# The third layer's first norm inside the second layer's last steps, and the first layer's diagonals on ScalarE

## The chip, the cores and the metric

The kernel runs on one core of one Trainium2 chip, in one launch. The metric is the device time of that launch in microseconds, the median of several runs. A profile of one execution stands beside it. The engines are TensorE (PE, with its weight loads as PEld), VectorE (DVE), ScalarE (ACT), GpSimd (POOL) and SyncE (SP), which here issues the plain DMAs.

## The reference

Four layers work on x of 4096 tokens by 256 values. Each normalises x and adds two branches, an attention and a feed-forward one:

```python
def _layernorm(x, axis=-1, eps=1e-05):
    m = jnp.mean(x, axis=axis, keepdims=True)
    v = jnp.var(x, axis=axis, keepdims=True)
    return (x - m) / jnp.sqrt(v + eps)
...
    x = L0_attn_x
    xn = _layernorm(x, axis=-1)
    x = x + _L0_attn_ref(xn, ...) + _L0_ffn_ref(xn, ...)
    xn = _layernorm(x, axis=-1)
    x = x + _L1_attn_ref(xn, ...) + _L1_ffn_ref(xn, ...)
...
```

The attention of the first layer is gated linear attention: a state per head, `S = S * exp(g_t) + k_t v_t`, read by `q_t @ S`. Its feed-forward branch is a mixture of 8 experts, the best two for each token:

```python
        w, idx = jax.lax.top_k(gate_logits, TOP_K)
        w = jax.nn.softmax(w, axis=-1)
...
        out = jnp.einsum('nec,ne->nc', y, comb)
```

The second layer has a selective scan (mamba) and a layer of retrieved experts (PEER, with rows gathered from tables). The third has a retention, whose core is a sigmoid of a product and a scan, with a feed-forward net behind it, and beside it a net of binary weights:

```python
        sig = jax.nn.sigmoid(jnp.einsum('bsh,hk->bsk', x, W_ret) + b_ret)

        def ema_step(carry, s_t):
            xi = 0.5 * s_t + 0.5 * carry
            return (xi, xi)
...
        w = jnp.where(kernel_bool, jnp.float32(1.0), jnp.float32(-1.0))
        return x @ w
```

The fourth is causal attention with 16 heads, and a root of two squared products.

## The kernel before

x stays on the chip, transposed: `xT` holds 128 partitions by 2 halves by 4096 tokens, and is worked on in 8 blocks of 512 tokens (`NB`, `BW`). Each layer is a function that returns one program for each engine. A program weaves the two branches of its layer: generators give their steps in turn, and where each step goes is set by paces (`weave`, L155; in the first layer `on_clock`, L168, through `weave_layer`, L508), in the second and third by tables of slots (`AT`, L1424 and L1979). So each engine's order is fixed when the program is built. At the end of a layer every engine goes through `layer_end` (L384), which waits for the last tick of every stage of the layer; SyncE issues the loads of the next layer behind it. Nearly all products go through one helper, `chain`, at L184, so that line stands for most of TensorE's rows.

**First layer's end.** The last expert tile is written to memory (`ys_slots`), and then the results come back by token: for each of `NC` = 32 groups of 128 tokens SyncE fetches two rows per token into `Gy` (L531, 8 buffers), and TensorE adds the two, weighted, with a product by a diagonal matrix for each: `wd`, 18 buffers of [128, 2, 128]. The diagonals are `ident` times a weight from `w8`. GpSimd makes them (L1288), one instruction for a pair, as soon as the last expert product (`y`, `TILES - 1`) is done, since `Gy` and `wd` lie in the memory `FW` in which the experts' weights were. VectorE adds the result to x (L1070). The last steps of the linear attention run in between: VectorE's `S` update (L857), TensorE's products, ScalarE's copies of `ob` (L1128), squares (L1134), gates (L1140), logarithm and exponential (L1146, L1150).

**Second layer's end.** Block 7 of the scan ends with `out_of(7)`: on TensorE a product of `u` with `mWo`, two halves of 4 matmuls each, which the trace shows as 16 passes; on VectorE two additions of it to x (L1605) and two of the residual (L1610). Behind it comes the last token group of PEER: transposes of `hg` (L1571), products with `hgT` and with diagonals made on ScalarE (L1866), and VectorE's weighted sums (L1764) and last addition to x (L1776). PSUM has three banks for this branch, `psm`, used in turn.

**Third layer's start.** Behind the barrier SyncE loads rW, vec, k0, W1, W2 and k1 in this order (L2043 to L2048). The norm of blocks 0 and 1 goes one step after another over three engines: sum of the two halves (L2009, VectorE), mean by a product with `onesm` (L1998, TensorE), subtraction (L2014), squares (L2028, ScalarE), their sum (L2019), variance (L2004, TensorE), table load, logarithm, exponential (L2035 to L2040, ScalarE), scaling (L2023, VectorE; that of block 1 behind the first scans). Then come the cast of x to `xa` (L2286), the signs of k0 (L2057, read from `bh`), the product with rW, the sigmoid (L2337) and the scan (L2193). The norms of later blocks stand inside the loop over blocks and aren't touched. Buffers: `sqs` were `sq_` and a part of `fa`; `both_` held the half sums.

## Time and profile before

| | us |
|---|---|
| median of 3 runs | 3743.24 |
| lowest, highest | 3740.03, 3744.06 |
| profiled execution | 3738.18 |
| its span | 3736.0 |

The profile is of one execution, and its moments are counted from the start of the span; what lies around the span in that run is 2.18 us. The mean granted clock of TensorE over the span is 0.962. TensorE is busy for 93% of the span, VectorE for 66%, ScalarE for 46% and GpSimd for 32%. Such shares are means over four layers with different limits. What a change in one place is worth is read from that place: the chain of work that ended last gives, step by step, what each piece of time was spent on, and the timeline what the other engines did beside it. The number in brackets behind a row is the time in which its engine was idle before it, with what ended that.

### The profile page before, as it was taken

What the parts mean: (1) busy time and instruction counts of PE and PEld (TensorE: products, weight loads), DVE (VectorE), ACT (ScalarE), POOL (GpSimd) and SP (SyncE); (2) the same over time, 40 slices, a digit from 0 to 9 for tenths busy, and PEclk for the clock granted to TensorE, in tenths of its full rate; (3) what the DMA queues carried; (4) which work ended last, traced back from release to release, by engine and by line L of the source; (5) the groups of instructions that cost most, each with busy time, mean ns of one, the idle gap of its engine ahead of it and who ended that gap; (6) DMA issues with size and microseconds to landing.
All of it is one profiled execution on the core that took longest, in us unless ns stands there. A gap on an engine that the chain in (4) does not pass through costs nothing.

```text
span 3736.0 us, 48136 instructions
## 1 busy us (share of the span) xinstructions
PE 3458.4 (93%) x16660; PEld 2069.5 (55%) x16660; DVE 2456.5 (66%) x6314; ACT 1727.1 (46%) x3243; POOL 1193.7 (32%) x1229
## 2 busy tenths in 40 slices
PE   9889999998999998999879999999799999999998
PEld 6556778776555555555546677777443333433332
DVE  5553344344799999999965434443568888788884
ACT  3333442332334433344334544444247676667667
POOL 0023334332455556555632322322221111011111
PEclk9889999999999999999989999999899999999999
DMA  2014555544476667766740000000111111111100
GB/s 81 33 61 154 186 186 189 183 141 169 150 216 203 209 203 219 214 203 208 233 148 3 1 1 1 1 0 1 44 22 29 25 26 34 33 31 31 35 18 23
DMA packets 105971, 368.88 MB, mean 99 GB/s; under 512 B 26736, under 2 KB 39680, under 8 KB 95744
## 3 DMA queue, kind: packets, MB, share of 16 engines
q0 software_dynamic: 58000, 303.74, 25.2%
q1 hardware_dynamic: 46640, 59.98, 5.8%
q8 instruction: 132, 2.16, 0.2%
q10 hardware_dynamic: 1088, 2.10, 0.2%
q14 instruction: 111, 0.91, 0.1%
HBM read 322.59 MB, written 17.69 MB: 91 GB/s over the span
## 4 chain that ended last, share of the span: by engine, by line
PE 70%; DVE 18%; ACT 7%; issue 3%; POOL 1%; DMA 1%; POOLq 0%; DVEq 0%; SPq 0%; ACTq 0%
PE ps L184 54%; PE ps L2710 6%; DVE mi L1687 2%; ACT P L2991 2%; PE ps L1552 2%; DVE hacc L1727 2%; DVE gathB L1764 2%; DVE pm L2858 2%; PE ps L2171 1%; DVE mx L1683 1%; PE ps L594 1%; DVE tm L1641 1%; DVE ps L2861 1%; PE ps L619 1%; PE ps L584 1%
## 5 line engine op out<-in xcount | busy, mean ns | idle before, releaser
L2991 ACT ACTIVATE P<-ps 128x512 f32<-128x512 f32 (+3 forms) x1280 | 587.9, 545 | 202.5 <-PE ps L184 200.2
L2858 DVE TENSOR_REDUCE pm<-ps 128x1 f32<-128x512 f32 x768 | 485.0, 683 | 72.9 <-PE ps L184 68.0
L1905 POOL DMA_INDIRECT gathB<-in_tab,idx x256 | 286.5, 1119 | 313.7 <-PE ps L1552 243.5
L184 PE MATMUL ps<-KS,QS 63*128 63x512 f32 (+3 forms) x1280 | 341.7, 412 | 16.8 <-ACT P L2991 5.5
L3048 POOL TENSOR_SCALAR_AFFINE_SELECT P<-P 128x256 f32<-128x256 f32 x256 | 102.9, 407 | 675.5 <-ACT P L2991 670.0
L1905 POOL DMA_INDIRECT gathA<-in_tab,idx x256 | 267.7, 1046 | 152.0 <-issue 77.4
L2710 PE MATMUL ps<-P,Va 128*32 128x512 f32 (+3 forms) x2560 | 302.7, 545 | 7.1 <-POOL P L3048 4.2
L184 PE MATMUL ps<-QS,KS 64*128 64x512 f32 (+3 forms) x1280 | 281.6, 423 | 1.5
L184 PEld LDWEIGHTS ps<-QS,KS 64*128 64x128 f32 x1280 | 131.6, 186 | 253.9 <-ACT P L2991 104.1
L2861 DVE CUSTOM_DVE_ANT_0 ps<-ps,past 128x128 f32<-128x128 f32 (+3 forms) x512 | 240.8, 513 | 36.3 <-PE ps L184 33.2
L184 PEld LDWEIGHTS ps<-KS,QS 63*128 63x128 f32 x1280 | 158.0, 186 | 168.5 <-ACT P L2991 80.4
L184 PE MATMUL ps<-f,K 128*128 128x512 f32 x1024 | 249.3, 395 | 0.0
L184 PE MATMUL ps<-WS,xn 128*128 128x512 f32 x512 | 231.2, 592 | 0.0
L184 PEld LDWEIGHTS ps<-f,K 128*128 128x128 f32 x1024 | 192.2, 188 | 46.8
L184 PE MATMUL ps<-moe,FW 128*128 128x128 f32 x1704 | 203.9, 277 | 0.8 <-ACT moe L1218 0.8
L184 PEld LDWEIGHTS ps<-moe,FW 128*128 128x128 f32 x1704 | 198.0, 194 | 1.1 <-ACT moe L1218 1.0
L1764 DVE CUSTOM_DVE_ANT_0 gathB<-hg,gathB,gte 128x512 f32<-128x512 f32 x256 | 178.1, 748 | 1.0 <-DMA gathB<-in_tab,idx 1.0
L1727 DVE SCALAR_TENSOR_TENSOR hacc<-gathA,lin,hacc 128x512 f32<-128x512 f32 x224 | 167.1, 746 | 3.5
L2432 POOL TENSOR_TENSOR f<-fa,f 128x512 fp32r<-128x512 f32 x64 | 85.3, 1333 | 258.8 <-DVE f L2304 258.8
L1246 POOL DMA_INDIRECT FW<-in_F,fidx x71 | 72.5, 1022 | 284.3 <-DVE moe L1051 156.0
L1057 DVE TENSOR_TENSOR moe<-moe,ps 128x384 f32<-128x384 f32 x71 | 39.3, 554 | 180.3 <-PE ps L184 116.6
L184 PEld LDWEIGHTS ps<-WS,xn 128*128 128x128 f32 x512 | 95.5, 190 | 111.4 <-issue 106.2
(392 smaller groups left out, 6952.2 us busy)
## 6 DMA issues: line engine op xcount, KB each, us to landing
FW<-ys_slots SPq DMA_DIRECT2D x32, 256.0 KB, 3.4
KS<-hi SPq DMA_DIRECT2D x256, 32.0 KB, 1.9
QS<-hi SPq DMA_DIRECT2D x256, 32.0 KB, 1.9
gathA<-in_tab,idx POOLq DMA_INDIRECT x256, 5.5
gathB<-in_tab,idx POOLq DMA_INDIRECT x256, 5.1
KS<-lo SPq DMA_DIRECT2D x128, 32.0 KB, 1.9
QS<-lo SPq DMA_DIRECT2D x128, 32.0 KB, 1.9
out<-xT SPq DMA_DIRECT2D x8, 512.0 KB, 3.2
```

The source lines that it names most:

```text
L184: m = pe.matmul(out, w, x, start=start and i == 0, stop=stop and i == len(pairs) - 1, skip_group_check=True)
L1552: pe.matmul(p[:, ms], GB[:, h, 512 + m * 128:640 + m * 128], dg[h], start=False, stop=h == 7, skip_group_check=True).then_inc(*PR.pe.tick( ...
L1687: v = dve.max_index(mi[:, 4 * g + i, :], mx[:, 4 * g + i, :], p[:, i * 128:(i + 1) * 128])
L1727: dve.scalar_tensor_tensor(out=hacc[:, :], in0=GA[:, h, 256:768], scalar=lin[:, h:h + 1], in1=src, op0=ALU.mult, op1=ALU.add).then_inc(*(P ...
L1764: dve.tensor_tensor_reduce(out=GB[:, h, 0:512], in0=hg[:, :], in1=GB[:, h, 0:512], scale=gt_[:, h:h + 1], scalar=0.0, op0=ALU.mult, op1=AL ...
L1905: pool.indirect_dma_start(out=(GA, GB)[half][:, h, :], out_offset=None, in_=d[f"tab{half}"], in_offset=bass.IndirectOffsetOnAxis(ap=idx[t ...
L2432: pool.tensor_tensor(f2[m % 2][:, 1, :], fa[:, (m + 2) % 3, :], f2[m % 2][:, 0, :].bitcast(F32), ALU.subtract).then_inc(*BN.pool.tick("f2" ...
L2710: m = pe.matmul(o_[32 * hd:32 * hd + 32, off:BW], Va[:, kt, h * 17:h * 17 + 32], Pb[2 * (kt % 2) + hd // 2][:, hd % 2, off:BW], start=kt = ...
L2858: v = dve.tensor_reduce(m, p, AX.X, ALU.max)
L2861: v = dve.tensor_tensor_reduce(out=p, in0=p, in1=past[:, 512 - w:512], scale=1.0, scalar=-3.0e38, op0=ALU.add, op1=ALU.max, accum_out=m)
L2991: act.activation(P_[:, hh, off:BW], psx.tile("s2", j, n, kt, pr, hh)[:, off:BW], ACT.Exp).then_inc(*psx.emptied(MN.act, "s2", j, n, kt, pr ...
L3048: pool.affine_select(out=P_, in_=P_, compare_op=ALU.is_ge, fill=0.0, base=0, pattern=[[0, 2], [1, 128]], channel_multiplier=-1).then_inc(* ...
```

## The change

It has two parts. In the first layer the diagonals are made by ScalarE, with two instructions for a pair in place of one of GpSimd, and are put at points of ScalarE's program between the attention's last steps, 14 groups ahead of their use. In the second and third, the norm of the third layer's blocks 0 and 1 is spread over the end of the second layer: the half sums in slot 8 of block 7, means and subtractions ahead of `out_of(7)`, sums of squares between its two additions, variances behind it, squares, roots and scalings at the ends of the programs of their engines. The buffers `both`, `xa`, `bh` and a new `rfirst` are placed in memory that is free by then. TensorE's program of the third layer begins with a wait for the logarithm of block 1.

```diff
@@ -768,7 +768,7 @@
                     p = psf.fill("moe", c)
                     pe.wait_all(psf.freed("moe", c))
                     for i in range(2):
-                        pe.wait_ge(*FF.pool.has("weight", c + i))
+                        pe.wait_ge(*FF.act.has("weight", c + i))
@@ -1229,8 +1229,23 @@
...
-                yield from delay(AFTER)
-                for _ in range(0, NC, 2):
+
+                def weights(c):
+                    act.wait_ge(*FF.dve.has("wb"))
+                    act.wait_ge(*FF.pe.has("y", TILES - 1))
+                    for i in range(c, c + 2):
+                        act.wait_ge(*FF.pe.has("moe", i - NWD))
+                        for s in range(2):
+                            a = act.activation(wd[i % NWD][:, s, :], ident[:, :], ACT.Copy, scale=w8[:, 2 + s, i:i + 1])
+                        a.then_inc(*FF.act.tick("weight", i))
+
+                yield from delay(1)
+                for c in range(0, 2 * AFTER - 2, 2):
+                    weights(c)
+                    yield
+                for c in range(0, NC, 2):
+                    if c + 2 * AFTER - 2 < NC:
+                        weights(c + 2 * AFTER - 2)
                     yield
 
@@ -1281,12 +1296,6 @@
...
-                pool.wait_ge(*FF.dve.has("wb"))
-                pool.wait_ge(*FF.pe.has("y", TILES - 1))
-                for c in range(NC):
-                    pool.wait_ge(*FF.pe.has("moe", c - NWD))
-                    pool.tensor_tensor(wd[c % NWD], ident[:, :].rearrange("p (o t) -> p o t", o=1).broadcast_to([128, 2, 128]),
-                                       w8[:, 2:4, c:c + 1].broadcast_to([128, 2, 128]), ALU.mult).then_inc(*FF.pool.tick("weight", c))
@@ -1510,7 +1519,9 @@
...
+                layers[2]["first means"][0](pe, psm)
                 out_of(NB - 1)
+                layers[2]["first variances"](pe, psm)
@@ -1605,6 +1616,8 @@
...
+                        if (n, m) == (NB - 1, 0):
+                            layers[2]["first rests"](dve)
@@ -1628,6 +1641,10 @@
...
+                    if n == NB - 1:
+                        dve.wait_ge(*PR.pe.has("rt", NT - 5, 3))
+                        dve.wait_ge(*PR.pe.has("hid", NT - 5))
+                        layers[2]["first halves"](dve)
@@ -1672,6 +1689,7 @@
...
+                layers[2]["first means"][1](dve, psm)
                 out_of(NB - 1)
@@ -1786,6 +1804,7 @@
...
                 weave((dve_mamba(dve), RATIO, LATE), (dve_peer(dve), 1.0))
+                layers[2]["first scales"](dve)
                 layer_end(dve, *names)
@@ -1848,6 +1867,7 @@
...
+                layers[2]["first squares"](act)
@@ -1897,6 +1917,7 @@
...
                 weave((act_mamba(act), RATIO, LATE), (act_peer(act), 1.0))
+                layers[2]["first roots"](act, psm)
                 layer_end(act, *names)
@@ -1928,7 +1949,13 @@
...
             xn = sb("xn2", [128, 2, 3 * BW])
+            both_ = sb("both", [128, BW])
             Wr = sb("rW", [128, 2, 256])
+            ph1 = ExitStack()
+            first = alloc(ph1)("rfirst", [128, 2, 2, BW])
+            ph1.close()
+            xa = sb("xa", [128, 2, 2, BW], F32R)
+            bh = sb("bh", [128, 2, BW])
@@ -1955,7 +1979,8 @@
...
-            sqs = [sq_, fa[:, 0:2, :]]
+            halves = [both_[:, :], bh[:, 0, :]]
+            sqs = [first[:, i, :, :] for i in range(2)]
@@ -1989,6 +2014,55 @@
                         yield
...
+            def pe_first_means(pe, ps):
+                for n in range(2):
+                    p = ps.fill("next", n, "mu")
+                    pe.wait_ge(*K.dve.has("ones"))
+                    pe.wait_ge(*LN.dve.has(n, "half"))
+                    pe.wait_all(ps.freed("next", n, "mu"))
+                    pe.matmul(p[:, :], onesm[:, :], halves[n], start=True, stop=True).then_inc(*LN.pe.tick(n, "mu"))
+
+            def pe_first_vars(pe, ps):
+                for n in range(2):
+                    p = ps.fill("next", n, "var")
+                    pe.wait_ge(*LN.dve.has(n, "rest"))
+                    pe.wait_all(ps.freed("next", n, "var"))
+                    pe.matmul(p[:, :], onesm[:, :], sqs[n][:, 0, :], start=True, stop=True).then_inc(*LN.pe.tick(n, "var"))
+
+            def dve_first_halves(dve):
+                for n in range(2):
+                    dve.wait_ge(*x_before(n))
+                    dve.tensor_tensor(halves[n], blk(xT, 0, n), blk(xT, 1, n), ALU.add).then_inc(*LN.dve.tick(n, "half"))
+
+            def dve_first_means(dve, ps):
+                for n in range(2):
+                    dve.wait_ge(*LN.pe.has(n, "mu"))
+                    dve.tensor_tensor(xr2(n), both(xT, n), ps.tile("next", n, "mu")[:, None, :].broadcast_to([128, 2, BW]),
+                                      ALU.subtract).then_inc(*ps.emptied(LN.dve, "next", n, "mu"))
+
+            def dve_first_rests(dve):
+                for n in range(2):
+                    dve_rest(dve, LN, (n,), sqs[n])
+
+            def dve_first_scales(dve):
+                for n in range(2):
+                    dve_scale(dve, LN, (n,), xr2(n), sqs[n])
+
+            def act_first_squares(act):
+                for n in range(2):
+                    act.wait_ge(*LN.dve.has("next", n, "mu"))
+                    act.activation(sqs[n], xr2(n), ACT.Square).then_inc(*LN.act.tick(n, "sq"))
+
+            def act_first_roots(act, ps):
+                for n in range(2):
+                    act.wait_ge(*LN.pe.has(n, "var"))
+                    if n == 0:
+                        act.preload_act_table_set(LN_EXP)
+                    act.activation(sqs[n][:, 0, :], ps.tile("next", n, "var")[:, :], ACT.Ln, bias=epsc[:, 0:1]).then_inc(
+                        *ps.emptied(LN.act, "next", n, "var"))
+                    act.wait_ge(*LN.act.has("next", n, "var"))
+                    act.activation(sqs[n][:, 0, :], sqs[n][:, 0, :], ACT.Exp, scale=-0.5).then_inc(*LN.act.tick(n, "rstd"))
@@ -2174,10 +2248,7 @@
...
-                for n in range(2):
-                    pe_mean(pe, LN, (n,))
-                for n in range(2):
-                    pe_var(pe, LN, (n,), sqs[n])
+                pe.wait_ge(*LN.act.has("next", 1, "var"))
@@ -2201,7 +2272,6 @@
...
                 scan(0)
-                dve_scale(dve, LN, (1,), xr2(1), sqs[1])
                 dve.wait_ge(*RT.act.has("W1"))
@@ -2312,12 +2382,6 @@
...
             def dve(dve):
-                for n in range(2):
-                    dve_half(dve, LN, (n,), both(xT, n), [], [LN.pe.has(n - 1, "mu")])
-                    dve_mean(dve, LN, (n,), both(xT, n), xr2(n), [])
-                dve_rest(dve, LN, (0,), sqs[0])
-                dve_rest(dve, LN, (1,), sqs[1])
-                dve_scale(dve, LN, (0,), xr2(0), sqs[0])
                 dve_split(dve, 0)
                 dve_signs0(dve)
@@ -2403,10 +2467,7 @@
...
                 table.clear()
-                for n in range(2):
-                    act_squares(act, LN, (n,), xr2(n), sqs[n], [])
-                for n in range(2):
-                    act_root(act, LN, (n,), sqs[n])
+                table["now"] = LN_EXP
```

ScalarE, the end of the first layer; `FW` is where `wd` lies, `ob`, `rms` and `gsil` are the attention's. Minus is before, plus is now:

```order
-L1128 ACTIVATE ob<-ps 128x4x128 x2
+L1239 ACTIVATE FW<-ident,w 128x128 x8
+L1128 ACTIVATE ob<-ps 128x4x128
+L1239 ACTIVATE FW<-ident,w 128x128 x16
+L1128 ACTIVATE ob<-ps 128x4x128
+L1239 ACTIVATE FW<-ident,w 128x128 x8
 L1134 ACTIVATE rms<-ob 128x512 x2
-L1140 ACTIVATE gsil<-ps 128x512 x4
+L1140 ACTIVATE gsil<-ps 128x512 x2
+L1239 ACTIVATE FW<-ident,w 128x128 x4
+L1140 ACTIVATE gsil<-ps 128x512 x2
+L1239 ACTIVATE FW<-ident,w 128x128 x12
```

Between the attention's copies, squares and gates there now stand groups of 4 to 16 diagonals.

VectorE, the end of the second layer and the start of the third, before:

```order
L1776 TENSOR_TENSOR xT<-xT,ps 128x2x128
L1605 TENSOR_TENSOR xT<-xT,ps 128x512 x2
L1610 TENSOR_TENSOR xT<-xT,xn 128x512 x2
L1764 ISA gathB,lin<-hg,gathB,gte 128x512
...
L1776 TENSOR_TENSOR xT<-xT,ps 128x2x128
L2009 TENSOR_TENSOR both<-xT 128x512
L2014 TENSOR_TENSOR xn<-xT,ps 128x2x512
L2009 TENSOR_TENSOR both<-xT 128x512
L2014 TENSOR_TENSOR xn<-xT,ps 128x2x512
L2019 TENSOR_TENSOR rsq<-rsq 128x512
L2019 TENSOR_TENSOR fa<-fa 128x512
L2023 TENSOR_TENSOR xn<-xn,rsq 128x2x512
```

and now (`rfirst` is the squares' buffer):

```order
L1794 TENSOR_TENSOR xT<-xT,ps 128x2x128
L2041 TENSOR_TENSOR xn<-xT,ps 128x2x512 x2
L1616 TENSOR_TENSOR xT<-xT,ps 128x512
L2093 TENSOR_TENSOR rfirst<-rfirst 128x512 x2
L1616 TENSOR_TENSOR xT<-xT,ps 128x512
L1623 TENSOR_TENSOR xT<-xT,xn 128x512 x2
L1782 ISA gathB,lin<-hg,gathB,gte 128x512
...
L1794 TENSOR_TENSOR xT<-xT,ps 128x2x128
L2097 TENSOR_TENSOR xn<-xn,rfirst 128x2x512 x2
L2356 CAST xa<-xn 128x1024
L2131 TENSOR_TENSOR K<-bh 128x1024 x2
```

The subtractions and the sums of squares moved ahead of the additions to x, and behind the last addition only the two scalings are left before the cast.

TensorE, the same place, before:

```order
L184 MATMUL ps<-u,mWo 128x512 x8
L1571 MATMUL ps<-ident,hg 128x128 x4
L184 MATMUL ps<-hgT,pWo 128x128 x4
L1552 MATMUL ps<-dg,gathB 128x128 x4
...
L1552 MATMUL ps<-hg,gathB 128x128 x4
L1998 MATMUL ps<-both,onesm 128x512 x2
L2004 MATMUL ps<-rsq,onesm 128x512
L2004 MATMUL ps<-fa,onesm 128x512
L184 MATMUL ps<-xn,rW 128x512 x4
```

and now:

```order
L1563 MATMUL ps<-hg,gathB 128x128 x4
L2024 MATMUL ps<-both,onesm 128x512
L2024 MATMUL ps<-bh,onesm 128x512
L184 MATMUL ps<-u,mWo 128x512 x8
L2031 MATMUL ps<-rfirst,onesm 128x512 x2
L1582 MATMUL ps<-ident,hg 128x128 x4
L184 MATMUL ps<-hgT,pWo 128x128 x4
...
L1563 MATMUL ps<-hg,gathB 128x128 x4
L184 MATMUL ps<-xn,rW 128x512 x4
```

The means stand ahead of the product with `mWo`, the variances behind it, and the third layer's first product on TensorE is the one with `rW`.

## Rows read from the trace of the kernel before

**Rows 1.** The page's part 4: engines' shares of the chain that ended last.

```profile
PE 70%; DVE 18%; ACT 7%; issue 3%; POOL 1%; DMA 1%; POOLq 0%; DVEq 0%; SPq 0%; ACTq 0%
```

**Rows 2.** The chain in order of time, first layer's end: start us, us, what.

```profile
842.12 9.34 issue
...
853.51 17.55 PE ps L184 x96
```

**Rows 3.** Timeline, VectorE and GpSimd there: start us, busy us, engine, line, operation, out<-in.

```profile
834.30 0.62 DVE L857 SCALAR_TENSOR_TENSOR S<-S,ebe,U 128x128 f32<-128x128 f32 x2
...
841.61 10.39 POOL L1288 TENSOR_TENSOR FW<-ident,w 128x256 f32<-128x256 f32 x18
...
841.79 10.37 DVE L857 SCALAR_TENSOR_TENSOR S<-S,ebe,U 128x128 f32<-128x128 f32 x2
```

**Rows 4.** Windows there: us, busy (x) of PE, PEld, DVE, ACT, POOL; PEclk, DMA share, GB/s.

```profile
840.10:841.80 1.70, 1.70 (x17) 1.69 (x16) 1.41 (x5) 0.00 (x0) 1.17 (x2) 1.00 0.00 0
...
853.50:856.89 3.39, 3.38 (x16) 3.39 (x17) 1.92 (x6) 0.00 (x0) 0.00 (x0) 0.53 0.00 0
...
842.00:893.00 51.00, 34.97 (x160) 23.08 (x159) 24.31 (x28) 11.98 (x19) 18.06 (x30) 0.87 0.34 106
```

**Rows 5.** Timeline, ScalarE at the first layer's end; in brackets the idle time before.

```profile
857.09 0.60 ACT L1128 ACTIVATE ob<-ps 128x512 f32<-128x512 f32 x1 [14.40 <-PE ps L184]
```

**Rows 6.** Tile FW (gathers), 835 to 860: issue to landing.

```profile
DMA to landing us min/median/max: 2.5/4.2/5.5
```

**Rows 7.** The chain in order of time, second layer's last block.

```profile
1834.41 3.33 DVE tm L1641 x5
```

**Rows 8.** Timeline, the second layer's tail.

```profile
1908.82 10.10 PE L184 MATMUL ps<-u,mWo 128*128 128x512 f32 x16 [5.03 <-DVE u L1598]
...
1915.59 0.69 DVE L1605 TENSOR_TENSOR xT<-xT,ps 128x512 f32<-128x512 f32 x1 [3.49 <-PE ps L184]
...
1918.96 0.69 DVE L1605 TENSOR_TENSOR xT<-xT,ps 128x512 f32<-128x512 f32 x1 [2.67 <-PE ps L184]
...
1926.26 1.28 ACT L1866 ACTIVATE hg<-ident,lin 128x128 f32<-128x128 f32 x4 [2.29 <-DVE lin L1764]
...
1933.04 0.42 DVE L1776 TENSOR_TENSOR xT<-xT,ps 128x256 f32<-128x256 f32 x1 [6.81 <-PE ps L1552]
```

**Rows 9.** The chain in order of time, the third layer's start.

```profile
1952.44 1.24 DVE re L2193
...
1956.63 1.14 DVE xn L2023
...
1968.03 3.37 DVE K L2062 x2
```

**Rows 10.** Timeline of that stretch; the last row is from tile bh, min/median/max ns.

```profile
1934.40 0.43 SPq L2045 DMA_DIRECT2D bh<-in_k  x1
...
1935.57 1.22 DVE L2014 TENSOR_TENSOR xn<-xT,ps 128x1024 f32<-128x1024 f32 x1 [1.28 <-PE ps L1998]
...
1946.59 6.54 PE L184 MATMUL ps<-xn,rW 128*128 128x512 f32 x8 [2.32 <-DVE xn L2023]
...
1950.43 1.28 ACT L2337 ACT_TABLE_LOAD   x1 [3.96 <-PE ps L184]
...
L2057 DVE TENSOR_TENSOR K<-bh x2: 1217/2290/3364, 1947.1 to 1948.3; 128x1024 fp32r<-128x1024 uint8 x2
```

**Rows 11.** DMA issues, 1933 to 1985: KB each, us to landing.

```profile
raw<-in_k SPq DMA_DIRECT2D x1, 1024.0 KB, 10.4
...
bh<-in_k SPq DMA_DIRECT2D x1, 512.0 KB, 4.6
...
rW<-in_rWr SPq DMA_DIRECT2D x1, 256.0 KB, 2.5
```

**Rows 12.** Windows, TensorE's clock in layers 2 and 3 (columns of rows 4).

```profile
1908.82:1914.82 6.00, 6.00 (x7) 2.52 (x8) 3.18 (x8) 1.91 (x2) 4.78 (x5) 0.50 0.84 269
...
1960.60:1970.00 9.40, 8.31 (x20) 5.00 (x20) 6.08 (x5) 5.89 (x9) 3.60 (x2) 0.71 0.00 0
...
1982.15:2012.80 30.65, 30.65 (x125) 24.68 (x126) 10.53 (x15) 10.61 (x17) 6.25 (x4) 0.94 0.03 9
```


## What I expect of it

> **What bounds the kernel now.** I read the chain of work that ended last first, by engine, to see who sets the time: TensorE 70% of the span, VectorE 18%, ScalarE 7%, and "issue", 3%, in which an engine waited for nothing that the profile shows [rows 1]. GpSimd has 1%. So work that leaves GpSimd pays only where GpSimd holds up another engine, and work that moves ahead pays only where TensorE or VectorE stood waiting. Then I read the same chain in order of time around the two places that the change touches, and beside it the timeline, which shows what the other engines did in that moment.
>
> At the end of the first layer the chain has a hole: VectorE's first update of the state `S` takes its usual third of a microsecond, then come 9.34 us of "issue", and only then do the second update and 17.55 us of TensorE work follow [rows 2]. The timeline has that pair at 10.37 us where the same pair, 7 us earlier, took 0.62; and exactly beside it lie 18 GpSimd instructions, the diagonals, 10.39 us back to back, 0.58 each [rows 3]. At the change from the second layer to the third the chain goes step by step through one norm, from the last addition to x at 1933.04 to the first scan of the retention at 1952.44 [rows 8, 9]. The sum is made against the profiled execution (3738.18 us), 5.06 us under the median of 3743.24.
>
> **Part 1, diagonals on ScalarE.** *Removed:* 32 GpSimd instructions. With them the cover of the hole goes. The second update would follow the first at 842.12 and end 9.34 us earlier; with the first one's share of the pair's excess (10.37 − 0.62) it is 9.7 us. *What is late next* is TensorE's work that uses `S`: it then starts after a pause of about a microsecond and not of eleven. After the long pause its first 16 matmuls of 128x128 took 3.38 us at a granted clock of 0.53; 17 such ones right before the hole took 1.70 at 1.00 [rows 4]. That is 1.6 us more. Against it, the gathered expert rows `Gy` are now wanted earlier: a gather lands 2.5 to 5.5 us after its issue [rows 6], and the first are issued about a microsecond after the last expert product, just behind the new need of the first pair, for which I charge 0.3. Sum: −9.7 − 1.6 + 0.3 = **−11.0** (bounds −8.5, when the gathers are waited for by 2.8 us, and −12).
>
> *Added:* 64 ScalarE instructions of 128x128. The nearest row has four of them at 1.28 us, 0.32 each [rows 8]: 20 us in all. ScalarE is busy for 11.98 of the 51 us from 842 to 893 [rows 4], and stood 14.40 us before the copy of `ob` at 857.09 [rows 5]; the first 32 diagonals (10 us) fit there, in the time in which the hole stood. The rest lie between two normalising steps, where ScalarE delays one by 4 × 0.32 = 1.3 us at most while VectorE has work of its own. I take 0; if none of it were covered it costs 20 us, the upper end, as a rival below. The last ten pairs are TensorE's and stay as they are.
>
> By the Trainium skill ("SBUF — State Buffer", section "Who interferes with whom") VectorE with two SBUF inputs and GpSimd reading SBUF lock one port pair for a whole instruction, and the other blocks until that one is finished. Taken by its words the hole would be one GpSimd instruction long, and this part would be worth 0.6 instead of 9.7; the rows show the wait going on through 16 or so of them, so I follow the rows and keep the rule's result as the first rival.
>
> **Part 2, the norm inside the second layer's tail.** *Moved to VectorE's slot 8 of block 7:* two additions of 128x512 (`halves`), at 0.69 each by the row of the same shape [rows 8]: 1.4. VectorE is on the chain there: 3.33 us of `tm` at 1834.41 [rows 7], with TensorE waiting. So these count in full but for rounding: **+1.3** (0 to +1.4).
>
> *Moved to the tail, in program order:* two mean matmuls before the output product. TensorE idles 5.03 us before it [rows 8], and the means need only the halves: covered. Two subtractions of 128x1024, 1.22 each [rows 10], before the first x addition: VectorE idles 3.49 there, 2.4 covered. Two `rests` of about 0.69 between the two x additions: idle 2.67 [rows 8], covered. The squares on ScalarE come behind the last gelu and are done before the product is. The two variances stand on TensorE behind the output product, ahead of the transposes of `hg`: 1.1 to 1.7 us, and those transposes feed products that anyway wait for diagonals made by ScalarE at 1926.26, before which ScalarE idled 2.29. The roots (table load 1.28 [rows 10], two logarithms and two exponentials at 0.60, the row of the nearest ScalarE shape [rows 5]) come behind ScalarE's last diagonals at 1927.54 and end about 1931.3, before VectorE's last addition at 1933.04, for which VectorE idles 6.81 [rows 8]. I take **0** for all of it. Ends: +5 if subtractions, rests and variances all come onto the path (2.4 + 1.4 + 1.7, less the slack of one), and −3 if TensorE, now idle for only some 3.3 us ahead of the output product, keeps its full clock: the first 6.00 us of that product ran at 0.50 [rows 12].
>
> **Part 3, the third layer's start.** *Gone from the path:* halves, means, subtractions, squares, rests, variances, roots. What is left from the end of the last addition (1933.46): two scales (2 × 1.22) to 1935.9 and the cast to `xa`, 0.7, to 1936.6. From there two branches meet at the first scan. TensorE: the weights rW, issued at once after the barrier, land 2.5 us later [rows 11], 1936.1, so its product starts there. The first output takes 4 of the 8 passes that took 6.54 us [rows 10]; I take half and a little more, 3.8, since the first ran at the lower clock: 1939.9, then table load 1.28 and one sigmoid 0.7: 1941.9. VectorE: the signs of k0 (2 × 1.22 undisturbed) wait for a load issued at 1934.40 that lands after 4.6 us [rows 10, 11], 1939.0; one of the two was stretched to 3.36 beside GpSimd's own first step [rows 10]. GpSimd's step now starts before the load lands, so I leave 0.8 of that: 1942.3. The scan starts at 1942.4 and not at 1952.44 [rows 9]: −10.0. Behind the two scans the second block's scale, 1.14, has gone from the chain too [rows 9]: −11.1. *What is late next:* raw key bytes of 1024 KB land 10.4 us after issue [rows 11], 1946.5; they are first read 15.6 us behind the first scan's start, at 1968.03 [rows 9], in the new time near 1957. Sum **−11.1** (−8 if the loads, now the last to come, take 3 us more; −12 without GpSimd's disturbance). The rest of the third layer has the same order of instructions, so the shift stays.
>
> **Sum:** −11.0 + 1.3 + 0 − 11.1 = −20.8. In the profiled frame 3717.4; against the median 3743.24 − 20.8 = **3722.4**.
>
> **The rivals.**
>
> (a) *The hole isn't GpSimd's run.* Then something else that starts at the same moment holds `S`, the eight gathers for one, or GpSimd's part in it is one instruction, 0.6. For it: the gathers too are in flight in the hole. Against: the hole ends with the 18th diagonal, to 0.2 us. The first part gives 0.6: 3743.24 − 0.6 + 1.3 − 11.1 = 3732.8. This is also the case that the edit doesn't do what it says. Chance 0.10.
>
> (b) *The norm's steps come onto the path of the tail:* VectorE and TensorE there have idle times of 2.7 to 5.0 us, but each such idle ends the moment that a result comes, and a step that starts late pushes what follows. +5 and 2 us less at the handover: 3743.24 − 20.8 + 7 = 3729. Chance 0.14.
>
> (c) *TensorE stays warm* ahead of the output product: −3, 3719.4. Chance 0.08.
>
> (d) *ScalarE becomes the bound at the first layer's end:* its queue is in order, and diagonals that wait for a freed buffer hold up the normalising steps behind them. With all 20 us exposed, 3742.4. Against it: 39 us of idle in the window. Chance 0.04.
>
> (e) *Slower:* one mechanism, the clock. In the third layer's first block TensorE works at 0.71 from 1960.60 on and at 0.94 over 30.65 us from 1982.15 [rows 12]; the new timing of its pauses there could leave it at the lower level, 0.50, until the next one. 8.31 × (0.71/0.50 − 1) + 30.65 × (0.94/0.50 − 1) = 3.5 + 27 = 30.5 us: 3722.4 + 30.5 = 3753. It decides for slower once over 28 us are lost. Against it: the pauses ahead of that stretch get shorter, not longer. Chance 0.02.
>
> **How the numbers follow.** My forecast, all three sums about as above, has the remaining 0.62. The likeliest time is 3722.4. Its own bounds are 3743.24 − 12 − 2 − 12 = 3717 and 3743.24 − 8.5 + 5 − 8 = 3732; runs of the same kernel lie up to 3 us from the median, so the range begins at 3714. It ends at 3733 to take in (a) and (b); only (d), (e) and the outsides are left out. A measurement of this kernel can tell 0.2% from no change, 7.5 us: faster means below 3735.7. Forecast, (a), (b) and (c) lie below it, 0.94 together, but (a) and (b) at once would give about 3740, for which I take off 0.02: faster 0.92, same 0.06, slower 0.02.
>
> **What would show it.** Step 1 is right if the two updates of `S` take 0.6 to 0.7 us, with no "issue" of several us behind the first, and the 16 matmuls behind them run at a clock near 1.0; wrong, by (a), if the pair is still near 10 us, and by (d) if TensorE's products of the last pairs wait for ScalarE's diagonals. Step 2 is right if the second layer's tail from the start of the output product to the last x addition takes as long as before (1908.82 to 1933.04, 24 us); wrong by (b) if the subtractions stand in the chain. Step 3 is right if the first scan starts 9 us after that last addition and not 19. If k0's signs stand in the chain with a wait for the load of over 4.6 us, the loads were the term that I mis-sized.

## The result, and the profile after

| | before | after |
|---|---|---|
| median us | 3741.64 (3732.95 to 3747.90, 6 runs) | 3715.43 (3714.22 to 3724.15, 6 runs) |
| ratio after / before | | 0.9936, 95% interval 0.9924 to 0.9947 |
| profiled execution us | 3738.18 | 3724.15 |
| its span us | 3736.0 | 3722.4 |

The change makes the kernel 0.64% faster (0.53% to 0.76%), 26.2 us by the medians (0.4 us of it outside the span, 2.2 us before and 1.8 after). A second measurement, of 6 and 13 runs, gave 3718.32 against 3740.74, a ratio of 0.9940 (0.9926 to 0.9953), 22.4 us. The forecast was 20.8 us less, 3722.4; its range, 3714 to 3733, holds both.

The profiled execution of after is the slowest of its six, 8.7 us above their median, so one profile alone would tell of 13.6 us. To see where time goes I compare the start of the same TensorE matmul, by its number in the program, in two traces; "lag" is after less before. The kernel was profiled once more (`again`, below), and its parts alone.

| lag us at | after | again | diag_only | norm_only | run_held |
|---|---|---|---|---|---|
| 826, ahead of the hole | +5.8 | −0.7 | +0.1 | −0.1 | −0.3 |
| 860, behind it | −4.9 | −11.7 | −10.7 | −0.1 | −10.6 |
| 917, second layer's start | −4.8 | −11.4 | −10.5 | −0.1 | −10.6 |
| 927, 10 us later | −1.5 | −8.1 | −7.2 | −0.1 | −10.6 |
| 1823, block 7, ahead of the half sums | −1.0 | −7.4 | −6.6 | −0.1 | −10.5 |
| 1843, behind them | −0.3 | −6.8 | −6.6 | +0.6 | −10.5 |
| first load of the third layer (1933.56) | −3.7 | −7.7 | −6.8 | −0.3 | −10.3 |
| 2033, third layer, behind its first block | −15.0 | −20.4 | −6.7 | −13.0 | −10.3 |
| 3716, near the end | −13.6 | −24.0 | −2.6 | −13.2 | −5.2 |

(The first column has the moment in the kernel before. `diag_only` is the first part of the change alone, `norm_only` the norm alone, `run_held` the kernel before with GpSimd's run started later; all three are below.)

*The hole.* The chain in order of time of the kernel after, the same place as [rows 2] (start us, us, what):

```profile
840.37 0.35 DVE S L857
...
848.90 2.88 DMA FW<-ys_slots
851.78 0.14 issue
851.91 14.25 PE ps L184 x80
```

and its timeline there, beside [rows 3], with ScalarE's diagonals:

```profile
840.10 0.61 DVE L857 SCALAR_TENSOR_TENSOR S<-S,ebe,U 128x128 f32<-128x128 f32 x2
...
844.18 2.45 ACT L1239 ACTIVATE FW<-ident,w 128x128 f32<-128x128 f32 x8 [0.70 <-PE ps L184]
...
847.60 0.61 DVE L857 SCALAR_TENSOR_TENSOR S<-S,ebe,U 128x128 f32<-128x128 f32 x2
...
848.39 4.77 ACT L1239 ACTIVATE FW<-ident,w 128x128 f32<-128x128 f32 x16
```

The pair that took 10.37 us takes 0.61. The "issue" of 9.34 us is gone from the chain, and what TensorE waits for next is the first gather, 0.33 us in all. The 16 matmuls that stood behind the hole follow a pause of 0.84 us now, and run at the full clock (column PEclk of the windows, the third from the right), where [rows 4] had 3.38 us at 0.53:

```profile
849.53:851.60 2.07, 2.02 (x16) 1.86 (x16) 1.93 (x6) 2.07 (x8) 0.00 (x0) 1.00 0.65 222
```

*The second layer's tail*, timeline of after, beside [rows 8]:

```profile
1907.53 8.54 PE L184 MATMUL ps<-u,mWo 128*128 128x512 f32 x16 [2.72 <-DVE u L1609]
...
1910.71 2.35 DVE L2041 TENSOR_TENSOR xn<-xT,ps 128x1024 f32<-128x1024 f32 x2
...
1913.57 1.51 DVE L2093 TENSOR_TENSOR rfirst<-rfirst 128x512 f32<-128x512 f32 x2
...
1915.90 1.88 PE L2031 MATMUL ps<-rfirst,onesm 128*128 128x512 f32 x4
...
1924.71 1.28 ACT L2061 ACT_TABLE_LOAD   x1
...
1929.37 0.42 DVE L1794 TENSOR_TENSOR xT<-xT,ps 128x256 f32<-128x256 f32 x1 [5.99 <-PE ps L1563]
```

Subtractions and sums lie beside TensorE's product, the roots end at 1928.6, ahead of the last addition. None of them stands in the chain.

*The third layer's start*, the chain in order of time, beside [rows 9]:

```profile
1929.37 0.43 DVE xT L1794
...
1930.73 4.05 DMA bh<-in_k
1934.81 2.60 DVE K L2131 x2
...
1937.53 1.24 DVE re L2264
```

The first scan starts 8.2 us behind the last addition's start, where it started 19.4 us behind it.

### The profile page after: what moved, and what is told of

The parts are those of the page before. It is cut to its first block, busy times and chain, and to the rows that moved or that the text cites. A ratio compares the mean times of both kernels' runs of the same rounds, so it can differ in the third digit from the quotient of the medians.

```text
span 3722.4 us, 48171 instructions
## 1 busy us (share of the span) xinstructions
PE 3463.3 (93%) x16660; PEld 2075.2 (56%) x16660; DVE 2442.8 (66%) x6314; ACT 1745.8 (47%) x3307; POOL 1174.9 (32%) x1197
## 4 chain that ended last, share of the span: by engine, by line
PE 69%; DVE 19%; ACT 7%; issue 3%; POOL 1%; DMA 1%; SPq 0%; POOLq 0%; DVEq 0%; ACTq 0%
PE ps L184 55%; PE ps L2774 6%; DVE mi L1705 3%; ACT P L3055 2%; DVE gathB L1782 2%; DVE hacc L1745 2%; PE ps L1563 2%; DVE pm L2922 2%; PE ps L2245 1%; DVE mx L1701 1%; PE ps L594 1%; DVE tm L1658 1%; DVE ps L2925 1%; PE ps L619 1%; PE ps L584 1%
```

## The experiments

Four of the runs (`norm_held`, `run_paced`, `run_of_9`, `gathers_held`) were made on another chip, where the kernel before takes 3781.33 us; their times are to be compared with each other and with that number. In all four TensorE falls some 30 to 33 us further behind in the second layer, in steps of 4 to 6 us, most of them ahead of the product with `mC`, once per block of the scan. Why that chip is slower there was not followed. The four last (`run_writes`, `update_psum`, `halves_late`, `warm_only`), one run each, stand beside one run of the kernel before, 3742.82 us.

### The kernel once more, and its parts alone

`again` is the changed kernel without an edit.

> The changed kernel, unaltered, profiled once more. Its first profile lies 8.7 us above the median of its runs; I put that down to that one execution: TensorE ran 5.7 us late already at 250 us, in the first layer's expert loads, and 3.3 us were lost at 924 to a longer stretch at the lower clock. Theory (disturbance of one execution): a profile near 3715, with no such lag at 250 us. Rival (the change itself delays these places, through the new places of its buffers or otherwise): the lag of 5.7 us at 250 us and the loss near 924 are there again, and the profile is near 3724.

Measured: 3718.32 us, ratio 0.9940 (0.9926 to 0.9953), profile 3712.0 us of span. The lag ahead of the hole isn't there (−0.7, where `after` has +5.8 from 250 us on), so it was that execution. The same 5.2 to 5.6 us stand at 59 us in the profiles of `halves_late`, `run_paced` and `gathers_held`, so it comes with either kernel. The loss of 3.3 us at the second layer's start is there again (−11.4 at 917, −8.1 at 927). So half of each theory held.

`diag_only` is the first part of the diff alone, on the kernel before:

```diff
-                        pe.wait_ge(*FF.pool.has("weight", c + i))
+                        pe.wait_ge(*FF.act.has("weight", c + i))
...
-                for c in range(NC):
-                    pool.wait_ge(*FF.pe.has("moe", c - NWD))
```

> Only the first part: diagonals on ScalarE, everything else as before. Theory (GpSimd's run holds VectorE's update of S): the pair of S updates near 841 takes 0.6 us instead of 10.37, TensorE gains 10.6 us by the end of the first layer, and the kernel is 10.6 us faster than before, ratio 0.9972. Rival (the parts help one another, or the gain is given back in the second layer): 5 us or less, ratio over 0.9986.

Measured: 3732.18 us, ratio 0.9975 (0.9961 to 0.9988), 8.6 us less. TensorE gains 10.8 us at the hole and loses 3.3 at the second layer's start.

`norm_only` is the other part alone, with GpSimd's diagonals (one line of the edit; the rest gives GpSimd its loop back):

```diff
-                        pe.wait_ge(*FF.act.has("weight", c + i))
+                        pe.wait_ge(*FF.pool.has("weight", c + i))
```

> Only the second part: the third layer's first norm in the second layer's end, diagonals on GpSimd as before. Theory: +0.7 to +1.3 for the half sums in block 7, -2 to -3 in the tail since TensorE's output product runs at the full clock for some 3 us more, -11.4 from the barrier to the second block of the third layer, together -13 to -14, ratio 0.9964. The forecast had -9.8 for it. Rival (the tail's gain in the profile was chance): -10 to -11, ratio 0.9972.

Measured: 3725.48 us, ratio 0.9961 (0.9948 to 0.9974), 15.3 us less, 13.2 in the profile. Half sums +0.7, tail −0.9, handover −12.7. So the parts add up: 8.6 and 15.3 make 23.9, both together gave 22.4 and 26.2.

### Who holds the update of S

`run_held` leaves the diagonals on GpSimd and only starts the run later:

```diff
                 pool.wait_ge(*FF.dve.has("wb"))
+                pool.wait_ge(*AT.dve.has("S", NB - 1, 3))
```

> The kernel before, but GpSimd's run of diagonals waits for the last update of S. Theory (the run is what holds the update): the pair of S updates near 841 takes 0.6 us and TensorE goes on some 9 to 10 us earlier; the diagonals are made some 4 us behind it and TensorE may wait 1 to 2 us for the first of them; 7 to 10 us faster than before, ratio 0.9978. Rival (the eight gathers or something else holds the update): the pair takes 10 us still, and the time is the same as before or longer.

Measured: 3728.72 us, ratio 0.9965 (0.9953 to 0.9977), 12.0 us less. Its timeline:

```profile
841.45 0.61 DVE L857 SCALAR_TENSOR_TENSOR S<-S,ebe,U 128x128 f32<-128x128 f32 x2
...
844.78 0.61 DVE L857 SCALAR_TENSOR_TENSOR S<-S,ebe,U 128x128 f32<-128x128 f32 x2
...
845.49 13.87 POOL L1289 TENSOR_TENSOR FW<-ident,w 128x256 f32<-128x256 f32 x24 [4.23 <-DVE S L857]
```

The update takes 0.61 us once the run isn't beside it, with the gathers issued from 842.76 on as ever. TensorE waits 0.75 us for the first diagonal. One line of waiting gives as much as making the diagonals on ScalarE (12.0 and 8.6 us, with intervals that overlap).

`gathers_held` does the opposite: the run as before, the gathers later.

```diff
+                sp.wait_ge(*AT.dve.has("S", NB - 1, 3))
                 for c in range(NC):
                     sp.wait_ge(*FF.pe.has("moe", c - NGY))
```

> The kernel before, but the gathers of the experts' results wait for the last update of S; GpSimd's run is as before. Theory (GpSimd's run): the pair of S updates takes 10.4 us as before, and TensorE waits a further 2 to 4 us for the first gather. Rival (the gathers hold the update): the pair takes 0.6 us.

Measured: 3789.29 us, one run (before 3781.33 there). No gather is in flight, and the pair takes the same time, to a hundredth:

```profile
851.75 10.40 POOL L1289 TENSOR_TENSOR FW<-ident,w 128x256 f32<-128x256 f32 x18
851.93 10.37 DVE L858 SCALAR_TENSOR_TENSOR S<-S,ebe,U 128x128 f32<-128x128 f32 x2
```

TensorE's lag grows by 3.7 us at that place: 1.6 by the start of the first product with a gathered row, the rest behind it, where its granted clock is still 0.50. Rival (a) has fallen in its first form: the owner is GpSimd's run.

`run_of_9` makes the run shorter:

```diff
-            NWD = 18
+            NWD = 9
```

> The kernel before with 9 buffers for diagonals instead of 18, so GpSimd's first run is 9 instructions long. Theory (VectorE's update waits for the end of the run): 9 x 0.577 = 5.2 us, the pair at 5 us, TensorE's gain by the first layer's end 5 us if the later diagonals, made one by one as buffers come free, are not waited for. Rival (gathers or another owner): the pair stays at 10 us.

Measured, one run: 3771.67 us. The pair takes 5.20 us beside a run of 5.24, and TensorE gains 4.1. In each of these pairs it is the second update that waits (9.75 us beside 18, 4.58 beside 9); the first, begun 0.2 us behind the run's start, takes its usual third of a microsecond:

```profile
849.91 5.24 POOL L1288 TENSOR_TENSOR FW<-ident,w 128x256 f32<-128x256 f32 x9
850.10 5.20 DVE L857 SCALAR_TENSOR_TENSOR S<-S,ebe,U 128x128 f32<-128x128 f32 x2
```

`run_paced` leaves the length and takes away only that the instructions follow each other without a gap:

```diff
                     pool.wait_ge(*FF.pe.has("moe", c - NWD))
+                    pool.wait_ge(*FF.pool.has("weight", c - 1))
```

> The kernel before, but each GpSimd diagonal waits for the end of the one before it, so the run has small gaps. Theory (a back-to-back run of GpSimd instructions keeps the shared port and VectorE gets no turn): with gaps VectorE gets in after the first, the pair of S updates takes under 2 us, TensorE goes on some 9 us earlier. Rival (GpSimd's work as such blocks it, gaps or not): the pair takes as long as the run of 18, 10 us or over.

Measured, one run: 3768.99 us.

```profile
848.74 14.70 POOL L1289 TENSOR_TENSOR FW<-ident,w 128x256 f32<-128x256 f32 x21
848.93 1.28 DVE L857 SCALAR_TENSOR_TENSOR S<-S,ebe,U 128x128 f32<-128x128 f32 x2
850.25 2.67 DVE L830 TENSOR_SCALAR Ss<-S,ebm 64x128 f32<-64x128 f32 x4
```

With GpSimd nearly as busy (0.61 us of work in every 0.70 now, against a new instruction every 0.58 before), the pair takes 1.28 us, about one GpSimd instruction over its 0.61, and TensorE gains 7.6. The scalings behind the pair are held too, 0.59 to 0.69 us each and not 0.29. So it isn't GpSimd's work as such: it is the run without gaps, in which VectorE gets no turn. By the Trainium skill ("SBUF — State Buffer", section "Who interferes with whom") the instruction that issues second blocks until the first has finished. With gaps that describes what is seen. Back to back it does not: the wait lasts to the end of the run, in runs of 9 and of 18.

`run_writes` has GpSimd only write; it leaves out the diagonals' values:

```diff
-                    pool.tensor_tensor(wd[c % NWD], ident[:, :]..., w8[:, 2:4, c:c + 1]..., ALU.mult).then_inc(...)
+                    pool.memset(wd[c % NWD], 1.0).then_inc(*FF.pool.tick("weight", c))
```

> The kernel before, but GpSimd fills the 18 diagonal buffers by memset, which reads nothing from SBUF (the diagonals are left out, so the experts' sum is wrong). The Trainium skill ("SBUF - State Buffer", section "Who interferes with whom") says that VectorE with two SBUF inputs contends with a GpSimd instruction that reads SBUF and not with one that only writes it. Theory (reading is what holds the update): the pair of S updates takes 0.6 us beside the run. Rival (any busy run of GpSimd holds it): the pair takes as long as the run of memsets.

`update_psum` leaves GpSimd as it was and changes VectorE's side. It leaves out the scaling of the product that goes into S, and a memset of one column follows each update:

```diff
-                    i.then_inc(*psa.emptied(AT.dve, "u", n, c))
-                    dve.wait_ge(*AT.dve.has("u", n, c))
                     dve.wait_ge(*AT.dve.has("Ss", n, c))
                     for j in range(2):
                         i = dve.scalar_tensor_tensor(out=S_[:, j, :], in0=S_[:, j, :], scalar=ebe[:, j, c:c + 1],
-                                                     in1=U2[:, j, :], op0=ALU.mult, op1=ALU.add)
+                                                     in1=p[:, j * 256:j * 256 + 128], op0=ALU.mult, op1=ALU.add)
-                    i.then_inc(*AT.dve.tick("S", n, c))
+                    i.then_inc(*psa.emptied(AT.dve, "u", n, c))
+                    dve.wait_ge(*AT.dve.has("u", n, c))
+                    dve.memset(scr[:, :], 0.0).then_inc(*AT.dve.tick("S", n, c))
```

> The kernel before, but VectorE's update of S takes its second tensor from PSUM in place of U in SBUF (a part of the product, not scaled, so the state is wrong), and a one-column memset follows it. GpSimd's run is as before. Theory (VectorE's second SBUF input is what meets GpSimd's reads): each update near 841 takes under 0.5 us and TensorE goes on 9 to 10 us earlier. Rival (any work of VectorE on S is held): one update takes 9.7 us.

Measured, one run each: 3735.97 and 3742.71 us, beside 3742.82 of before. The timelines, first of `run_writes`, then of `update_psum`:

```profile
841.35 4.64 POOL L1288 MEMSET FW<- 128x256 f32 x18
841.55 0.61 DVE L857 SCALAR_TENSOR_TENSOR S<-S,ebe,U 128x128 f32<-128x128 f32 x2
842.20 4.76 DVE L830 TENSOR_SCALAR Ss<-S,ebm 64x128 f32<-64x128 f32 x4
```

```profile
845.09 10.35 POOL L1289 TENSOR_TENSOR FW<-ident,w 128x256 f32<-128x256 f32 x18
845.16 0.61 DVE L856 SCALAR_TENSOR_TENSOR S<-S,ebe,ps 128x128 f32<-128x128 f32 x2
...
845.93 10.20 DVE L831 TENSOR_SCALAR Ss<-S,ebm 64x128 f32<-64x128 f32 x4
```

In both the update of S goes through beside the run in 0.61 us: it is held where VectorE takes two tensors from SBUF and GpSimd reads SBUF, and neither of the two alone is enough. The same section of the Trainium skill says that a VectorE instruction with two SBUF inputs contends with a GpSimd instruction that reads SBUF and not with one that only writes it. That agrees. But the expected gain came only in part, or not at all: the next instruction, the scaling `Ss` from SBUF to SBUF (four in 1.17 us undisturbed), is now the one that waits, 4.76 us beside the memsets and 10.20 beside the products. The Trainium skill says there that `tensor_scalar` can enter a mode that uses both port pairs and contends with GpSimd. The rows agree, for GpSimd's writes too. I had looked at one victim and missed the next in the same queue. TensorE gains 4.8 us in `run_writes` and nothing in `update_psum`.

### The loss at the second layer's start

`norm_held` is the norm part with `run_held`'s wait:

```diff
+                pool.wait_ge(*AT.dve.has("S", NB - 1, 3))
```

> The changed kernel's norm part, with the diagonals back on GpSimd and their run held until the last update of S. Three profiles with ScalarE's diagonals have a stretch at the lower TensorE clock of 10.2 us near the second layer's start, three without have 3.4 us there, which is 3.3 us of TensorE's time. Theory (it belongs to ScalarE's diagonals): 3.4 us here too, and a time 3 us under the changed kernel's, ratio 0.993. Rival (chance of the single executions): the stretch may be either, and the time is the changed kernel's within 2 us, ratio 0.994.

Measured: 3757.25 us against 3781.33 there, ratio 0.9935 (0.9917 to 0.9952). That is the changed kernel's ratio, with an interval that can't tell 2 us. But its profile has the short stretch, 3.4 us. Windows of TensorE's clock at that place, first before, then after (column PEclk, the third from the right):

```profile
917.00:921.00 4.00, 4.00 (x14) 2.21 (x14) 0.18 (x1) 2.31 (x4) 0.00 (x0) 0.64 0.98 412
921.00:925.00 4.00, 4.00 (x28) 3.25 (x27) 2.04 (x3) 1.27 (x3) 0.00 (x0) 0.93 1.01 422
```

```profile
912.00:916.00 4.00, 4.00 (x16) 2.34 (x16) 0.18 (x1) 2.52 (x4) 0.00 (x0) 0.71 0.97 408
916.00:920.00 4.00, 4.00 (x20) 3.88 (x19) 1.29 (x2) 1.39 (x3) 0.00 (x0) 0.50 1.00 420
920.00:924.00 4.00, 4.00 (x11) 2.45 (x11) 1.33 (x2) 0.00 (x0) 0.00 (x0) 0.51 1.03 381
```

The stretch at the lower level lasts 10.2 us in `after`, `again` and `diag_only`, with ScalarE's diagonals, but also in `run_of_9`, with GpSimd's, and TensorE loses the same 3.3 us there in `halves_late` and in `run_writes`. It is 3.4 us in the kernel before, `norm_only`, `run_held`, `norm_held`, `run_paced`, `update_psum` and `warm_only`. TensorE's instructions at that place are the same in all, in the same order. So the long stretch comes without ScalarE's diagonals too, though all four profiles with them have it; what decides it stays open. Only the changed kernel was profiled twice, and both times had the long one, so it isn't shown either that one kernel can have both.

### The second layer's tail

`halves_late` moves the half sums:

```diff
-                    if n == NB - 1:
-                        ...
-                        layers[2]["first halves"](dve)
...
+                layers[2]["first halves"](dve)
                 layers[2]["first means"][1](dve, psm)
```

> The changed kernel with the two half sums moved from slot 8 of block 7 to VectorE's program just ahead of the subtractions. Theory (they cost 1.2 us at once in block 7 and 0.7 net): no step of TensorE's lag at 1840, the means on TensorE then come some 1.4 us later, still ahead of the output product or delaying it by up to 2 us, so the second layer ends within 1.5 us of the changed kernel's. Rival (the half sums cost nothing where they are, and the step of 1.2 us is chance): the step at 1840 stays.

Measured, one run: 3727.07 us. The step of TensorE's lag is gone (−0.8 at 1823, −0.9 at 1843; with the half sums there, it grows by 0.6 to 0.7), so the 0.7 us are theirs. But the tail is far longer than I expected. From the chain in order of time and the timeline:

```profile
1910.79 0.41 DVE xT L1793
1911.20 0.61 DVE both L2035
1911.82 0.04 issue
1911.86 3.78 PE ps L2023 x4
```

```profile
1911.86 2.07 PE L2023 MATMUL ps<-both,onesm 128*128 128x512 f32 x2 [10.69 <-DVE both L2035]
...
1915.43 7.95 PE L184 MATMUL ps<-u,mWo 128*128 128x512 f32 x16
```

VectorE comes to the half sums only behind its weighted sums of gathered rows (`hacc`, until 1910.8) and an addition to x. TensorE has stood idle for 10.69 us by then; it makes the means ahead of the output product, which starts at 1915.43 and not near 1908, and the third layer's loads start at 1937.1. Against the changed kernel, from the same place in block 7, that is 7.0 us lost (+4.3 of lag from 1823 to the third layer's first load, where `after` has −2.7), with the 0.7 saved counted in. Against `again` and `norm_only`, whose output product had less of the full clock, it is 4.6 and 4.5; by 2033, against the three, 3.7 to 4.9. In block 7 the half sums are cheap, since they are long done when TensorE asks for the mean.

`warm_only` puts two products ahead of the last output product, on the kernel before:

```diff
+                        if (n, m) == (NB - 1, 0):
+                            pe.wait_all(psm.freed("mamba", n, m))
+                            for i in range(2):
+                                pe.matmul(p[:, :], onesm[:, :], Wu[...], start=True, stop=True)
                         pe.wait_ge(*MA.dve.has("y", n, 3))
```

> The kernel before with two more TensorE products of 128x512 (their result is overwritten) ahead of the last output product of the second layer, and nothing of the norm. Theory (the products in the pause keep the clock up for the output product, which took 10.10 us before and 8.54 in the changed kernel): it takes 8.5 to 8.9. Rival (its clock changes from one execution to the next, since profiles without the norm have 8.6 to 10.2 as well): anything from 8.5 to 10.2, and no rule.

Measured, one run: 3742.83 us, beside 3742.82 of before. The output product took 10.13 us. The edit did not shorten the pause, though: the two products (1.88 us) ran right behind 48 PEER products that took 5.8 us there and 7.3 in the kernel before, and the pause ahead of the output product is 5.08 us where it was 5.03. So this run alone says only that two more products ahead of the same pause change nothing. The other profiles say more:

| | pause ahead of it us | output product us | from its start to the third layer's first load |
|---|---|---|---|
| before | 5.0 | 10.10 | 24.7 |
| diag_only | 5.0 | 10.18 | 24.9 |
| run_held | 7.3 | 9.70 | 24.2 |
| run_writes | 6.5 | 9.86 | 24.4 |
| update_psum | 6.7 | 8.56 | 22.4 |
| warm_only | 5.1 | 10.13 | 24.8 |
| run_paced | 2.4 | 8.62 | 22.5 |
| run_of_9 | 2.9 | 8.60 | 22.4 |
| gathers_held | 3.2 | 10.14 | 24.8 |
| after | 2.7 | 8.54 | 22.4 |
| again | 3.7 | 9.73 | 23.8 |
| norm_only | 3.8 | 9.69 | 23.7 |
| norm_held | 2.0 | 8.83 | 22.8 |

It takes 8.5 to 9.7 us with the norm's steps and 8.6 to 10.2 without them, and `after` and `again` are the same kernel with 8.54 and 9.73. So the norm's steps alone do not decide it, and the gain that the profile of `after` has there is mostly absent in `again`. The rival's "no rule" goes too far, though: behind a pause under 3 us the product took 8.5 to 8.8 us (7.95 in `halves_late`, with no pause), behind one of 3.2 us or more 9.7 to 10.2, with one exception, `update_psum`. No run changed the pause alone, so that is a pattern and not a shown cause. The whole tail goes with the product. Less the product, the tail is 13.8 to 14.0 us with the norm and 13.8 to 14.7 without: the norm's steps cost nothing there.

## Why the prediction was right, step by step

**Part 1, −11.0.** The profiles have −10.7 in `after`, −11.0 in `again`, −10.8 in `diag_only` (table of lags, 826 to 860). Its terms hold. The pair gave 9.76 us, where the forecast had 9.7. The 16 matmuls behind it went from 3.38 us to 2.02, so the clock gave 1.36 and not 1.6 (the forecast took 1.60 us for them at the full clock). The first gather was waited for by 0.33 us in `after` and 0.05 in `again`, where it had 0.3. The 64 diagonals on ScalarE hid nearly as forecast: 8 took 2.45 us, 0.31 each. Four of them stand in the chain, between the squares and the logarithms of the attention's norm (chain of after, in order of time), and TensorE's pause there is 4.61 us in `diag_only` where it was 4.20, so 0.4 us show. In return 0.65 us came back just ahead of it: two VectorE steps of the attention (`ob`) that had taken 1.0 us each beside GpSimd's diagonals took 0.7.

```profile
872.48 0.63 ACT rms L1134
873.11 1.17 ACT FW L1239 x4
874.27 1.15 ACT rms L1146 x2
```

The cause was named rightly, and is shown: the hole went with the run's start (`run_held`), its length (`run_of_9`) and its gaps (`run_paced`), and stayed without the gathers (`gathers_held`). Rival (a) had a chance of 0.10, and the Trainium skill's rule taken by its words was the reason; the rows had spoken against it.

**Not foreseen:** 3.3 us at the second layer's start, at the lower clock. With it this part gave 8.6 us by the medians and not 11.0. `run_held`, without that loss, gave 12.0; the intervals of the two overlap.

**Part 2, +1.3 for the half sums.** Right in kind, mis-sized: 1.2 us at once, of which 0.5 is won back within 15 us, so +0.6 to +0.7 net in three profiles: what TensorE lost there it made up in part, and the forecast counted the 1.3 in full. **The tail, 0,** was right in its mechanism: every step lies in the idle time that was named for it. The profiles have −0.9, −0.9 and −3.4 there. In `after` 1.6 of the 3.4 lie in the output product, at its clock, 1.0 ahead of it and 0.8 behind. Rival (c), 3 us from a TensorE that keeps its clock, came in one profile of three; `again` is the same kernel without it. Rival (b) did not come; `halves_late` shows how near it was, 4.5 to 7 us, had one step been some instructions later.

**Part 3, −11.1** (−10.0 up to the first scan, −1.1 behind it). Mis-sized on the small side: −11.3 in `after`, −12.7 in `again`, −12.7 in `norm_only`. Two branches meet at the first scan, as the forecast had it. In `after` the signs end last: k0 landed after 4.05 us where I had taken 4.6, and the two took 2.60 where I had 3.2, so the scan starts 8.2 us behind the addition's start and not 9.4 (1933.04 to 1942.4 in the forecast); that is −11.2 up to the scan and −0.1 behind it. In `again` and `norm_only` TensorE's product ends last, at the lower clock, with 3.77 us, the number that I took; there the scan starts 9.4 us behind the addition's start, as forecast: −10.0 up to the scan, and −2.7 behind it, where the forecast had −1.1. From the chain of `again`:

```profile
1928.89 3.77 PE ps L184 x4
1932.75 1.28 ACT L2401
1934.04 0.70 ACT re L2401
1934.76 1.24 DVE re L2264
```

The stretch from the first scan to the matmul at 2033 ran at a granted clock of 0.87 before, 0.89 in `after` and 0.93 in `again` and `norm_only`. The windows, first of before, then of `again`:

```profile
1952.44:2033.00 80.56, 67.98 (x242) 49.07 (x241) 47.39 (x56) 39.08 (x53) 20.93 (x13) 0.87 0.01 4
```

```profile
1934.76:2012.60 77.84, 64.24 (x242) 46.11 (x241) 46.25 (x55) 39.23 (x54) 20.94 (x13) 0.93 0.06 22
```

So in `again` and `norm_only` the term that was too small is the one behind the scan. The forecast counted only the scaling that is gone from VectorE, 1.1 us. TensorE is busy for 64.2 us there and not 68.0, with the higher clock; how much of the other 1.6 us is the clock's was not taken apart, and in `after`, with the scaling gone too, the stretch is no shorter than before.

**The sum.** −20.8 against −22.4 and −26.2 by medians. Terms by profile of `again`: −11.0 (hole), +3.3 (clock), +0.6 (half sums), −0.9 (tail), −12.7 (handover) make −20.7; small steps in between give back 1.0, and from −0.7 ahead of the hole the lag comes to −20.4 at 2033. Near the end −24.0 stands; the last 3.6 us came in the fourth layer, where `diag_only` and `run_held` lost 4 and 5 us against the kernel before, and were not followed. So the forecast's closeness is in part two misses that cancel: 3.3 us of loss not seen, and some 2.5 us more of gain in the tail and the handover. By the medians the misses are larger: part 1 gave 8.6 us where 11.0 was forecast, and the norm 15.3 (9.7 to 19.5) where 9.8 was. The slower rival (e) had nothing in the profiles for it; (d) neither.

## What to carry to other kernels

Look for VectorE instructions whose duration is far off that of their like, and for what GpSimd does beside them: a run of GpSimd instructions without gaps holds a VectorE instruction with two SBUF tensors to the end of the run, and one wait that starts the run later is as good as moving the work to another engine (12.0 and 8.6 us, with intervals that overlap). Gaps within it gave 7.6 of some 11 us in one profile. Freeing one VectorE instruction alone may only pass the wait on to the next, as in `update_psum`. A norm at a layer's seam is worth the sum of its hops less what arrives next, here loads of 2.4 and 4 us issued only at the seam. Put steps that another engine waits for well ahead of the place where they are needed: 0.7 us paid early saved 4.5 to 7 up to the next layer's first load.

## What the runs showed of the hardware

- A VectorE instruction of 0.35 us waited to the end of a run of 18 GpSimd instructions without gaps (9.75 us), and of 9 (4.58 us); with each GpSimd instruction waiting for the end of the one before, the longest took 0.77 us.
- GpSimd's memsets (18 in 4.64 us) did not hold `scalar_tensor_tensor` with two SBUF tensors, and held one `tensor_scalar` from SBUF to SBUF for 3.87 us.
- TensorE's clock at one place of the same program differs between executions: the product of 16 passes took 8.54 and 9.73 us in two executions of the changed kernel, and 7.95 to 10.18 over all fourteen profiles. The pause ahead of it was 2.7 us in the first of the two and 3.7 in the second. The stretch at the second layer's start cost 3.3 us more in six of the fourteen than in the kernel before; whether one kernel can have both isn't shown. One execution of the changed kernel lay 8.7 us above the median of six.
